# Queries and keys kept in DRAM in the order of the partitions that read them: four writes and one read per tensor in place of one or two writes and eight reads

## What is computed

```
x = LN(attention_A(q from x, k and v from ctx; 16 heads of 64) @ Wo + bo + x)        # layer 0
x = LN(x + attention_B(q, k, v from x; 16 heads of 16; mask_SxS) @ o_w + o_b)        # layer 1
x = LN(x + attention_C(q from x, k and v from ctx; 16 heads of 16) @ co_w + co_b)
x = LN(x + relu(x @ lin1_w + lin1_b) @ lin2_w + lin2_b)
attention: softmax(q k^T / sqrt(head size), masked) v
```

## Time and profile before

| | |
|---|---|
| median of 3 runs | 2088.13 us (2084.88 to 2092.41) |
| the profiled execution's own time | 2080.84 us |
| its span | 2079.1 us |
| PE busy | 1893.7 us (91%) |
| DVE, ACT, POOL busy | 64%, 58%, 47% |
| mean granted clock of PE | 0.97 |
| DMA moved | 135.94 MB, 145109 packets, 139760 of them under 2 KB |
| reads per tensor k_B, q_B, k_C, q_C | 128 of 128 KB; median landing 5.2, 9.7, 4.4, 4.8 us |

### The profile page before, as it was taken

How to read it: one execution, slowest core, us unless ns; L and a number is a source line. 1 busy time by engine, 2 the same in 40 slices (tenths; PEclk the granted TensorE clock), 3 DMA queues, 4 the chain that set the end, 5 groups by cost and what they waited for, 6 DMA issues and landing times.

```text
span 2079.1 us, 42825 instructions
## 1 busy us (share of the span) xinstructions
PE 1893.7 (91%) x12608; PEld 1451.6 (70%) x12608; DVE 1326.9 (64%) x5194; ACT 1196.1 (58%) x3985; POOL 984.2 (47%) x1014
## 2 busy tenths in 40 slices
PE   3999999999999999999899999999999999986776
PEld 2776777777776777777677777767777777764554
DVE  1465676766767676666767666676766667664642
ACT  1454766556565665656666565666656566663632
POOL 0233555536364553645455464544546464552622
PEclk8999999999999999999999999999999999998988
DMA  7032525171422517143260714326071422507120
GB/s 209 28 61 58 87 64 82 33 118 33 77 43 59 92 33 118 33 73 46 54 97 33 119 32 72 47 54 97 32 118 33 80 39 64 86 21 117 25 42 6
DMA packets 145109, 135.94 MB, mean 65 GB/s; under 512 B 23280, under 2 KB 139760, under 8 KB 144880
## 3 DMA queue, kind: packets, MB, share of 16 engines
q1 hardware_dynamic: 141760, 132.97, 35.6%
q10 hardware_dynamic: 3120, 0.01, 0.1%
HBM read 90.99 MB, written 41.94 MB: 64 GB/s over the span
## 4 chain that ended last, share of the span: by engine, by line
PE 64%; issue 16%; POOL 8%; DVE 7%; SPq 2%; ACT 1%; DMA 1%; POOLq 0%; DVEq 0%; ACTq 0%
PE ps_gd L472 27%; PE ps_t L608 10%; PE ps_ga L472 9%; PE ps_s L591 9%; POOL prob L959 7%; PE ps_av L633 5%; PE ps_av L642 4%; DVE prob L868 2%; PE ps_ga L478 1%; DVE res_ln L826 1%; DVE res_ln L844 1%; DVE stats_ln L829 1%; POOL res_ln L947 1%; ACT k_ctx L685 1%; POOL rstd_ln L924 1%
## 5 line engine op out<-in xcount | busy, mean ns | idle before, releaser
L959 POOL TENSOR_TENSOR prob<-prob,recip 128x512 f32<-128x512 f32 x768 | 788.9, 1048 | 927.3 <-DVE recip L879 926.1
L698 ACT ACTIVATE prob<-prob,ext 128x256 f32<-128x256 f32 x1536 | 757.9, 501 | 23.4 <-DVE ext L868 23.3
L705 ACT ACTIVATE prob_t<-ps_t 128x512 f32<-128x512 f32 x384 | 229.2, 597 | 462.5 <-PE ps_t L608 462.4
L608 PE MATMUL ps_t<-ident,prob 128*128 128x128 f32 x3072 | 416.5, 277 | 38.1 <-POOL prob L959 22.7
L608 PEld LDWEIGHTS ps_t<-ident,prob 128*128 128x128 f32 x3072 | 357.4, 142 | 92.6 <-POOL prob L959 31.8
L884 DVE COPY prob_t<-ps_t 128x512 f32<-128x512 f32 x384 | 262.5, 684 | 174.7 <-PE ps_t L608 170.5
L698 ACT ACTIVATION_READ_ACCUMULATOR prob<-prob,ext 128x1 f32 x1536 | 296.9, 193 | 0.0
L868 DVE CUSTOM_DVE_ANT_0 prob<-ps_s,mask_a 128x256 f32<-128x256 f32 x512 | 186.7, 421 | 111.3 <-PE ps_s L591 108.2
L868 DVE CUSTOM_DVE_ANT_0 prob<-ps_s,mask_b 128x256 f32<-128x256 f32 x512 | 187.5, 419 | 73.9 <-PE ps_s L591 73.8
L868 DVE CUSTOM_DVE_ANT_0 prob<-ps_s,zero 128x256 f32<-128x256 f32 x512 | 185.7, 419 | 34.9 <-PE ps_s L591 34.7
L591 PE MATMUL ps_s<-k_ctx,q 64*128 64x256 f32 x1024 | 150.4, 413 | 24.8 <-DVE ext L868 16.2
(11 more groups left out here) (87 smaller groups left out, 2567.4 us busy)
## 6 DMA issues: line engine op xcount, KB each, us to landing
k_B<-k_parts_B SPq DMA_DIRECT2D x128, 128.0 KB, 5.2
q_B<-q_parts_B SPq DMA_DIRECT2D x128, 128.0 KB, 9.7
k_C<-k_parts_C SPq DMA_DIRECT2D x128, 128.0 KB, 4.4
q_C<-q_parts_C SPq DMA_DIRECT2D x128, 128.0 KB, 4.8
k_parts_C<-k_hl SPq DMA_DIRECT2D x16, 512.0 KB, 3.0
k_parts_B<-k_hl SPq DMA_DIRECT2D x16, 512.0 KB, 3.4
q_parts_B<-q_hl SPq DMA_DIRECT2D x32, 256.0 KB, 2.4
q_parts_C<-q_hl SPq DMA_DIRECT2D x32, 256.0 KB, 11.5
```

The source lines that it names most:

```text
L608: last = nc.tensor.transpose(two(ps_t[e])[:, kt, qt * P:(qt + 1) * P], src[:, e, qt, kt * P:(kt + 1) * P], ident[:, :])
L698: last = nc.scalar.activation(tile, tile, ACT.Exp, bias=ext[:, slot, e, t:t + 1], scale=-1.0, accum_out=sums[:, slot, e, t:t + 1])
L705: nc.scalar.activation(prob_t[:, body.slot(step, PT_RING), 0], two(ps_t[0]), ACT.Copy).then_inc(pt_act[s], 1)
L959: nc.gpsimd.tensor_tensor(rows, rows, recip[:, slot, e].unsqueeze(2) .to_broadcast([P, TT, TOK]), ALU.mult).then_inc(normed[s], 1)
```

## The change

The parts lie in DRAM in the order of the partitions of `k4` and `q4`: `k_parts` and `q_parts` get the shape (half e, part, row r, head c, token). Each part is written out whole, so the high and the low part are both written twice, by four DMAs of 256 KB per tensor with runs of 1 KB; one DMA of 1 MB then reads the tensor into all 128 partitions, with runs of 8 KB. For this a partition of `q_hl` and `k_hl` must hold row r, head c in the order 8 r + c. So the columns of the four weights for queries and keys of B and C are permuted once: they are loaded into the tiles of v_B, v_C, ctx_B and ctx_C, which are free at the start, and POOL copies them into place (16 copies of 128x128, `sort_weights`), after which it signals `w_sorted` to PE. The four biases are permuted by eight DMAs from DRAM to DRAM with elements of 4 bytes, put ahead of the weights of layer 1, and then loaded as columns. DVE's wait in `split` and SP's waits count four saves.

```diff
-        k_parts = {"B": nc.dram_tensor("k_parts_B", (1, 2, D, TOK), F32),
-                   "C": nc.dram_tensor("k_parts_C", (BATCH, 2, D, TOK), F32)}
-        q_parts = {s: nc.dram_tensor("q_parts_" + s, (2, D, TOK), F32) for s in "BC"}
+        k_parts = {"B": nc.dram_tensor("k_parts_B", (1, 2, PARTS, DH1, PAIRS, TOK), F32),
+                   "C": nc.dram_tensor("k_parts_C", (BATCH, 2, PARTS, DH1, PAIRS, TOK), F32)}
+        q_parts = {s: nc.dram_tensor("q_parts_" + s, (2, PARTS, DH1, PAIRS, TOK), F32) for s in "BC"}
...
-                sp.dma_start(k_parts["B"][0].rearrange("a (d p) t -> p (a d) t", p=P),
-                             k_hl[:, :, :, :].rearrange("p a d t -> p (a d) t")).then_inc(k_saved["B"], 16)
+                for part in range(PARTS):
+                    sp.dma_start(k_parts["B"][0, :, part].rearrange("e r c t -> (r c) e t"),
+                                 k_hl[:, part % 2]).then_inc(k_saved["B"], 16)
...
             def spread_keys(s, b):
-                sp.wait_ge(k_saved[s], count(b, 16, 16))
+                sp.wait_ge(k_saved[s], count(b, 16 * SAVES, 16 * SAVES))
...
-                by_pair = kept.rearrange("b a (e c r) t -> e a r (b c) t", e=2, r=DH1)
-                for part in range(4):
-                    for e in range(2):
-                        sp.dma_start(k4[s][rows_of(e, part), :, :].bitcast(F32), by_pair[e, part % 2]
-                                     ).then_inc(spread_k[s], 16)
+                rows = "e a r c t -> (e a r) c t" if s == "B" else "b e a r c t -> (b e a r) c t"
+                sp.dma_start(k4[s][:, :, :].bitcast(F32), kept.rearrange(rows)).then_inc(spread_k[s], 16)
 
             def spread_queries(s, b):
-                for a, split in enumerate((q_high[s], taken["qs" if s == "B" else "qc"])):
-                    sp.wait_ge(split, count(b, 1, 1))
-                    sp.dma_start(q_parts[s][a].rearrange("(d p) t -> p d t", p=P), q_hl[:, a, :, :]
-                                 ).then_inc(q_saved[s][a], 16)
+                for part in range(PARTS):
+                    if part % 2 == 0:
+                        sp.wait_ge((q_high[s], taken["qs" if s == "B" else "qc"])[part // 2], count(b, 1, 1))
+                    sp.dma_start(q_parts[s][:, part].rearrange("e r c t -> (r c) e t"), q_hl[:, part // 2]
+                                 ).then_inc(q_saved[s], 16)
                 if s == "B":
                     spread_keys(s, b)
...
+                sp.wait_ge(q_saved[s], count(b, 16 * SAVES, 16 * SAVES))
+                sp.dma_start(q4[s][:, :, :].bitcast(F32), q_parts[s].rearrange("e a r c t -> (e a r) c t")
+                             ).then_inc(spread_q[s], 16)
...
+            for n in sorted_bias:
+                for k in range(DT):
+                    sp.dma_start(sorted_bias[n][k].rearrange("(r c) -> r c", c=PAIRS),
+                                 io[f"{L1}{n}_b"].rearrange("(k c r) -> k r c", c=PAIRS, r=DH1)[k],
+                                 allow_slow_non_contiguous=True).then_inc(bias_sorted, 16)
...
-                    for saved in q_saved[s0] if name[0] == "q" else [k_saved[s0]]:
-                        dve.wait_ge(saved, count(b0, 16, 16))
+                    dve.wait_ge((q_saved if name[0] == "q" else k_saved)[s0], count(b0, 16 * SAVES, 16 * SAVES))
...
+            def sort_weights():
+
+                pool.wait_ge(w_in["attn1"], 16 * (len(w1) + 2))
+                for n, w in unsorted.items():
+                    for d in range(DT):
+                        for m in range(2):
+                            last = nc.gpsimd.tensor_copy(
+                                w1[n][:, d, m * P:(m + 1) * P].rearrange("p (r c) -> p r c", r=DH1),
+                                w[:, d, m * P:(m + 1) * P].rearrange("p (c r) -> p r c", r=DH1))
+                    last.then_inc(w_sorted, 1)
```

More of the change, by code:

```diff
@@ L255, in program @@
         own_ready = sem("own_ready")
+        w_sorted, bias_sorted = sem("w_sorted"), sem("bias_sorted")
         mask_read = sem("mask_read")
@@ L276, in program @@
         k_high = {s: sem("k_high_" + s) for s in "BC"}
-        q_saved = {s: [sem(f"q_saved_{part}_{s}") for part in ("high", "low")] for s in "BC"}
+        q_saved = {s: sem("q_saved_" + s) for s in "BC"}
         k_saved = {s: sem("k_saved_" + s) for s in "BC"}
@@ L294, in program @@
         column = lambda n: io[n].rearrange("(k p) -> p k", p=P)
+        sorted_bias = {n: nc.dram_tensor("bias_" + n, (DT, P), F32) for n in ("q", "k", "cq", "ck")}
         L0, L1 = "L0_xattn_", "L1_xattn_"
@@ L358, in save_cross @@
                 sp.wait_ge(taken["kc"], count(b, 1, 1))
[L359 to L361 removed]
+                for part in range(PARTS):
+                    sp.dma_start(k_parts["C"][bass.ds(b, 1), :, part].rearrange("b e r c t -> (r c) b e t"),
+                                 k_hl[:, part % 2].unsqueeze(1)).then_inc(k_saved["C"], 16)
                 sp.wait_ge(taken["vc"], count(b, 1, 1))
@@ new lines, in spread_keys @@
+                rows = "e a r c t -> (e a r) c t" if s == "B" else "b e a r c t -> (b e a r) c t"
+                sp.dma_start(k4[s][:, :, :].bitcast(F32), kept.rearrange(rows)).then_inc(spread_k[s], 16)
+            def spread_queries(s, b):
+                for part in range(PARTS):
+                    if part % 2 == 0:
+                        sp.wait_ge((q_high[s], taken["qs" if s == "B" else "qc"])[part // 2], count(b, 1, 1))
+                    sp.dma_start(q_parts[s][:, part].rearrange("e r c t -> (r c) e t"), q_hl[:, part // 2]
+                                 ).then_inc(q_saved[s], 16)
@@ L402, in spread_queries @@
                 if s == "B":
                     spread_keys(s, b)
-                for part in range(4):
-                    if part % 2 == 0:
-                        sp.wait_ge(q_saved[s][part // 2], count(b, 16, 16))
-                    for e in range(2):
-                        src = q_parts[s][part // 2].rearrange("(e c r) t -> e r c t", e=2, r=DH1)
-                        sp.dma_start(q4[s][rows_of(e, part), :, :].bitcast(F32), src[e]
-                                     ).then_inc(spread_q[s], 16)
+                sp.wait_ge(q_saved[s], count(b, 16 * SAVES, 16 * SAVES))
@@ L431, in _ @@
                              ).then_inc(w_in["small"], 16)
-            for n, src in (("q", "q_b"), ("k", "k_b"), ("cq", "cq_b"), ("ck", "ck_b"), ("l1", "lin1_b")):
-                sp.dma_start(col[n][:, :], column(L1 + src), allow_slow_non_contiguous=True
+            sp.dma_start(col["l1"][:, :], column(L1 + "lin1_b"), allow_slow_non_contiguous=True
+                         ).then_inc(w_in["small"], 16)
+            for n in sorted_bias:
+                sp.wait_ge(bias_sorted, 16 * DT * len(sorted_bias))
+                sp.dma_start(col[n][:, :], sorted_bias[n].rearrange("k p -> p k"), allow_slow_non_contiguous=True
                              ).then_inc(w_in["small"], 16)
@@ L912, in _ @@
             pool.wait_ge(dve_const, 2)
+            def sort_weights():
[7 more added lines that the diff above has]
+                    last.then_inc(w_sorted, 1)
             def job(body, step):
-                _, name, _, _ = step
+                _, name, i, _ = step
+                if body.present == {"x", "a"} and (name, i) == ("k", 3):
+                    sort_weights()
                 if name not in LN_AFTER:
```

17 lines of the change are left out of this document (8 added, 9 removed).

## The result

The changed kernel takes **2130.22 us** (median of 4 runs, 2127.65 to 2131.5) against 2086.51 us before (4 runs, 2083.13 to 2092.41): ratio 1.0205, 95% interval 1.0178 to 1.0232. The forecast was 2078.5 us, a little faster. The change makes the kernel 43.7 us slower. Of the runs of this document one, the fifth of e5_half_at_head, took 6863.95 us and is left out of its ratio; nothing on record says why.

The account below looks back on a forecast made before the run. PE was taken to bound the loop, with transfers showing only at the end and the third batch's C. -11.0 - 1.1 + 2.5 = -9.6 us on the median of 2088.13 gave 2078.5 us, range 2068 to 2092.

Parts of the forecast that it names:

- The drain: Last body, without stage a, where transfers are exposed on PE: C starts earlier, -11.0 us (bounds -8 to -15).
- the sign: Checks afterwards: q_B reads about 4.5 us from issue to landing; PE's gap before the end's first k_B scores under 3 us.
- The third batch: Start of the third batch's C: PE's wait of 1.09 us goes, -1.1 us.
- The loop, part (a): In the loop, DVE's split of C waits for four writes of q_B: taken as 0, bound +1 us x 12.
- The loop, part (b): Loop's head, PE idle 1.98 us and DVE 4.75 us: k_C's read ends sooner but is denser; taken as 0.
- rival 1: Loop's head gets worse, the dense read holding back what PE awaits: up to +33 us; chance 0.12 from +1.45 us a turn.
- rival 4: Loop's head: DVE's 5 us shrinks to 2, A's second scores start sooner: 2.2 us, 2076; inside the forecast's 0.67.
- The start: Before the loop: eight small bias DMAs ahead of the weights take SP's time, half hidden: +2.5 us (0 to +8).
- Rival 2: Start eats the gain: bias DMAs delay weights 6 us or more, or POOL copies exceed 0.6 us: 2086, chance 0.15.
- POOL's sorting: At the start, 16 copies of 128x128 take 5.6 us, hidden in POOL's 8.02 idle us: 0 (0 to +8).

Follow-up runs that it names:

- e5_half_at_head: The change, but only half of k_C (512 KB) read at the loop's head, the rest after DVE's first pair of attention A: 2103.28 us, ratio 1.0084.
- e3: The change, with the loop's k_C read waiting for DVE's first pair of A, and bias DMAs and loads behind the last weight: 2054.79 us, ratio 0.9858.
- e10: The change, with the loop's k_C read waiting for PE's first product of the new turn, and biases behind the last weight: 2053.05 us, ratio 0.9846.
- e2: The change, but the eight bias DMAs and four bias loads moved behind the last weight, with their own semaphore: 2109.55 us, ratio 1.0122.
- e4: The kernel before, with SP waiting in the loop for DVE's first pair of A ahead of its eight k_C reads: 2068.67 us, ratio 0.9914.
- e7: The change, but k_C read as eight DMAs into 16 partitions each, in runs of 8 KB: 2092.44 us, ratio 1.0038.
- e8: The kernel before, plus only the eight DRAM-to-DRAM bias DMAs of 4-byte elements ahead of layer 1's weights, results unused: 2098.27 us, ratio 1.0078.
- e9: The kernel before, plus eight DMAs of 1024 4-byte elements from DRAM into 128 partitions on chip, ahead of layer 1's weights: 2086.25 us, ratio 1.0002.

## Why the prediction was wrong

1. **The drain, -11.0: right.** Measured -10.3; from the save of K to the first scores of C it is 23.2 us (1940.44 to 1963.59) in place of 34.0 (1881.36 to 1915.33). That the size fits so well is luck in part, since the single sizes were off and cancelled or were covered. DVE's wait for the four saves grew to 4.02 us (forecast 2.03 + 2.2 = 4.2). The read ran at 317 GB/s in the loop, not 389, and q_B took 7.2 us to land (forecast 4.3; the sign asked for about 4.5), but PE was only ready at 1956.27, when the data of 1948.74 + 7.2 = 1955.9 was there. PE's gap in front of B fell from 11.08 us to none, where the sign asked for under 3.
2. **The third batch, -1.1: right in kind.** PE's wait for q_C is gone (0.74 us for DVE in its place); in the sum it cannot be seen behind the late start.
3. **The loop, part (a), DVE's wait for four saves, 0: right.** In the change the split of C waits 0.2 us for PE, and once 0.31 us for the saves. The real test is e3, where the turns are shorter: there DVE waits 1.6 to 3.6 us for the saves in eleven of the loop's turns, as in the row below, and a turn is within 0.3 us of that of e10, where it waits 0.6 us at most. So the wait is real, and PE pays next to nothing for it.

```profile
1038.64 0.69 DVE L818 TENSOR_TENSOR q_hl<-ps_gd,col_cq 128x512 fp32r<-128x512 f32 x1 [2.25 <-DMA q_parts_B<-q_hl]
```

4. **The loop, part (b), 0: the step that failed.** The prediction saw both gaps, saw that the read is denser, and chose 0 with "it ends sooner now" and, against rival 1, "the read is over by about 1030.5, when DVE arrives". That looked at DVE, and for DVE it was right: its gap fell from 4.9 us to 3.1, as rival 4 had it in kind, with no gain for PE that could be seen. PE comes to the branch 2.9 us behind the issue, in the midst of the dense read, and its instruction block left when the read had drained, 2.4 us behind the transposes in place of 0.4 us ahead. The old reads, slowly issued, left the line short at just this moment; their slowness, which the change removes, had kept PE's instructions out of the line. The price of rival 1 had a second hole: it counted the gap (up to 3 us; measured +2.2) and not the clock behind it. Longer idle time brought the fall to 1.2 GHz in every turn in place of six in eleven, another 1.6 us. Together that is 3.5 us a turn, 39 in eleven, more than the +33 that rival 1 had as its upper end at a chance of 0.12 for all above 1.45 us. The earlier trace rows had shown the same thing in the drain (0.64 behind 11 idle us), and the prediction used it there, not at the head.
5. **The start, +2.5 (0 to +8): far too small.** Measured +18.1 to the first store; 15.5 of it in PE's first scores. The eight DMAs were priced by what SP needs to issue small ones, as if the queue behind were as fast as for any other; the text itself noted that 4-byte writes to DRAM occur nowhere in the trace, and then took the end of the range from rows of another kind. Rival 2 named the right place, at 6 us and more. The last small load went out at 49.39, not at 36 to 39. Even with a loop at 0 the sum would have been near +8 (18.1 - 10.3).
6. **POOL's sorting, 0: right.** Four copies take 1.40 to 1.42 us, 0.35 each, done by 91.8, and the next product comes 2.63 us later, released by DVE. The Trainium skill ("GPSIMD Engine Reference", Performance pitfalls for Q7 kernels) had led to an estimate of 0.3.

```profile
90.38 1.40 POOL L925 COPY w_ck<-ctx_C 128x128 f32<-128x128 f32 x4
94.41 2.04 POOL L977 TENSOR_TENSOR prob<-prob,recip 128x512 f32<-128x512 f32 x2 [2.63 <-DVE recip L884]
```

Not settled: where the 1.4 us come from that stay with no data in front, and whether the start pays for the write of 4-byte elements into DRAM or for reading them 64 bytes apart. The clock's share is worked out from the windows; no run held the clock up with the gap left in.

## What to carry to other kernels

In this kernel the idle time at the loop's head that no releaser ends was a wait for instructions, and a dense transfer issued 1.9 us ahead of the last work before the branch stood in front of them. Look for the instruction queue beside such a gap, issue large reads behind the first product of the new turn, and price a longer gap with the clock that it costs behind it. A faster transfer is not harmless where it was hidden; ask what stood beside it that a dense one will hold up. A copy of 4-byte elements from DRAM to DRAM is best issued where nobody waits for the loads behind it, as in e2, and a kind of transfer that no row of the trace shows is to be priced with a wide upper end, or run alone first.

## What the runs showed that was not expected

- The kernel before had 1.5 us a turn to give at its loop's head, unrelated to the change: e4 is 0.9914 of it with one wait added.
- The clock fell behind the head in eleven turns of eleven with mean gaps of 3.1 and 4.2 us, in six or seven of eleven with 2.0 (before, e7, e8, e9), and in one or none with 1.4.
- Eight DMAs with 1024 elements of 4 bytes in all, 4 KB, cost 15 us of start when copied from DRAM to DRAM and 2 when brought on chip.
- Half of a dense read at the head cost 62% of what the whole cost in PE's gap (1.7 of 2.8 us), since it took 2.5 us to drain where the whole took 3.5.
